# Graph attention in split precision: the turned probabilities of a head pair in 64-row blocks, and the order of a pair's step

## The reference

```python
h = max(layernorm(x), 0)
q, k, v = h @ wq.T + bq, h @ wk.T + bk, h @ wv.T + bv
q2 = (q @ wiq.T + biq).reshape(384, 16, 64).transpose(1, 0, 2)     # k2, v2 alike
scores = einsum('hnd,hmd->hnm', q2, k2) / 8 + mask[None]
attn = softmax(scores, axis=-1)
out = einsum('hnm,hmd->hnd', attn, v2).transpose(1, 0, 2).reshape(384, 1024)
result = x + out @ wo.T + bo
```

## Time and profile before

| | before |
|---|---|
| median of 3 runs | 299.47 us |
| profiled execution, its own time | 299.46 us |
| span in that profile | 297.7 us |
| TensorE busy | 291.4 us, 98% |
| VectorE / ScalarE / GpSimd busy | 177.7 / 153.6 / 148.5 us |
| granted TensorE clock | 1.0 of full speed |
| transposes of probabilities | 144, of 128x128, 272 ns each, overlapping |

### The profile page before, as it was taken

One profiled execution on the slowest core, in us unless ns is written; L12 is line 12 of the kernel. 1 busy time (PEld: TensorE's weight loads), 2 busy tenths in 40 slices (PEclk: granted clock), 3 DMA queues, 4 the chain that ended last, 5 costly groups with the idle time before them and its releaser, 6 DMA issues.

```text
span 297.7 us, 4737 instructions
## 1 busy us (share of the span) xinstructions
PE 291.4 (98%) x1705; PEld 271.6 (91%) x1705; DVE 177.7 (60%) x475; ACT 153.6 (52%) x288; POOL 148.5 (50%) x153
## 2 busy tenths in 40 slices
PE   6999999999999999999999999999999999999996
PEld 3799998888899999999999999999999999888885
DVE  4995988786544443444467665656666666735241
ACT  2874642252532444334434586868686868975100
POOL 5551354643463545544400895657484839884000
PEclk9999999999999999999999999999999999999999
DMA  7948875648743444333554043040404040400032
GB/s 269 329 154 284 280 232 191 219 166 279 285 115 108 132 141 143 109 109 137 186 184 143 0 142 104 40 137 7 141 3 143 1 141 12 167 36 2 0 141 73
DMA packets 15818, 40.84 MB, mean 137 GB/s; under 512 B 3481, under 2 KB 4914, under 8 KB 15794
## 3 DMA queue, kind: packets, MB, share of 16 engines
q1 hardware_dynamic: 13346, 38.53, 38.9%
q0 software_dynamic: 2016, 1.21, 1.4%
q10 hardware_dynamic: 432, 0.79, 0.7%
HBM read 37.71 MB, written 2.81 MB: 136 GB/s over the span
## 4 chain that ended last, share of the span: by engine, by line
PE 89%; DMA 4%; DVE 3%; ACT 2%; issue 0%; POOL 0%; SPq 0%
PE bank L805 25%; PE bank L807 24%; PE bank L806 24%; PE bank L933 5%; PE bank L920 5%; PE bank L949 3%; PE bank L948 3%; DMA raw<-in_slabs 2%; DMA x_sb<-in_x 1%; ACT w_hi L433 1%; DVE stats L640 1%; ACT a_hi L463 1%; DMA key_rows<-key_row 1%; DVE a_lo L686 0%; ACT x_sb L453 0%
## 5 line engine op out<-in xcount | busy, mean ns | idle before, releaser
L386 POOL DMA_INDIRECT cells<-value,cell x51 | 53.1, 1042 | 63.8 <-DMA cells<-value,cell 46.8
L433 ACT ACTIVATE w_hi<-raw 128x1024 fp32r<-128x1024 f32 x51 | 54.1, 1060 | 22.2 <-PE bank L807 17.3
L805 PE MATMUL bank<-a_hi,w_hi 128*128 128x384 f32 x184 | 61.6, 335 | 0.7 <-DVE b_lo L661 0.7
L807 PE MATMUL bank<-a_lo,w_hi 128*128 128x384 f32 x184 | 61.5, 334 | 0.0
L806 PE MATMUL bank<-a_hi,w_lo 128*128 128x384 f32 x184 | 61.5, 334 | 0.0
L673 DVE TENSOR_TENSOR w_lo<-raw,w_hi 128x1024 fp32r<-128x1024 f32 x36 | 44.0, 1223 | 15.6 <-ACT w_hi L433 15.6
L412 POOL TENSOR_SCALAR prob<-prob,row_inv 128x384 f32<-128x384 f32 x36 | 22.7, 642 | 40.1 <-DVE row_inv L740 40.1
L357 POOL TENSOR_TENSOR w_lo<-raw,w_hi 128x1024 fp32r<-128x1024 f32 x15 | 35.9, 2395 | 7.1 <-ACT w_hi L433 7.1
L805 PEld LDWEIGHTS bank<-a_hi,w_hi 128*128 128x128 f32 x184 | 34.5, 188 | 1.1 <-DVE w_lo L673 1.0
L806 PEld LDWEIGHTS bank<-a_hi,w_lo 128*128 128x128 f32 x184 | 34.5, 188 | 0.0
L807 PEld LDWEIGHTS bank<-a_lo,w_hi 128*128 128x128 f32 x184 | 34.5, 188 | 0.0
(11 more groups left out here) (142 smaller groups left out, 609.2 us busy)
## 6 DMA issues: line engine op xcount, KB each, us to landing
raw<-in_slabs SPq DMA_DIRECT2D x56, 512.0 KB, 3.4
work<-key_rows SPq DMA_DIRECT2D x6, 256.0 KB, 6.2
prob<-key_rows SPq DMA_DIRECT2D x6, 256.0 KB, 3.8
x_sb<-in_x SPq DMA_DIRECT2D x3, 512.0 KB, 6.3
out_y<-x_sb SPq DMA_DIRECT2D x5, 256.0 KB, 2.1
cells<-prob SPq DMA_DIRECT2D x2, 576.0 KB, 7.4
cells<-value,cell POOLq DMA_INDIRECT x51, 3.8
x_sb<-in_x ACTq DMA_DIRECT2D x3, 256.0 KB, 4.4
```

What stands on the lines that cost most here:

```text
L386: nc.gpsimd.indirect_dma_start(out=cells[c][:, :], out_offset=bass.IndirectOffsetOnAxis(ap=cell[:, t:t + 1], axis=0), in_=value[:, t:t + 1 ...
L433: nc.scalar.activation(split_place(s)[0], raw[:, s % RAW, :], ACT.Copy).then_inc(slab_hi, 1)
L805: nc.tensor.matmul(psum, w[0], a[0], start=first, stop=False)
L807: return nc.tensor.matmul(psum, w[0], a[1], start=False, stop=last)
```

## The change

- For heads 0 to 11 (`in_halves`), both heads of a pair are turned in one run, `turn_pair`. Each transpose takes 64 rows of a block, so it uses one half of the array: 36 transposes, two by two on the two halves, each with a 64x64 identity moving. Results of the lower and the upper half go to different banks, so a turned block of 384 columns lies in two banks in runs of 64, and the copies read it by `pt_place` and write it in order by `pt_as_placed`.
- On TensorE the key tile stands whole behind the scores; then come the values of the pair before's odd head, the run of transposes, 3/8 of the query tile, the values of the even head, 5/8 of the query tile. The odd head's values wait for the next step.
- On ScalarE all six exponentials stand in a row, then a weight split and the key tile. `half_part` and the copies come after these. VectorE and GpSimd follow the same order.
- The psum banks are one tensor and renumbered; `scores` waits for `pt_lo` of the head two back, the copies for both half banks and for the values that read the buffer before, and the waits of `tile` and of the first `heads_values` are moved by two tiles.
- The last four heads keep the old transposes.

```diff
-            return bank[((0, 1, 7), (2, 5, 6))[h % 2 if h < H - 4 else 0][m]]
+        def in_halves(h):
+            return h < H - 4
+        def pt_place(h, m):
+            if not in_halves(h):
+                return bank[m][:, 0:N]
+            own = slice(h % 2 * NT * D, (h % 2 + 1) * NT * D)
+            return banks[:, 2 * m:2 * m + 2, own].rearrange("p x (n d) -> p x n d", d=D)
...
             def pt_hi_part(h, m):
-                act.wait_ge(pt_done, h * NT + m + 1)
-                nc.scalar.activation(pt_hi[:, m, :], pt_bank(h, m)[:, 0:N], ACT.Copy).then_inc(pt_hi_ok, 1)
+                if in_halves(h):
+                    both = h // 2 * 2 * NT + 2 * (m + 1)
+                    act.wait_ge(pt_done, both)
+                    act.wait_ge(pt_done_high, both)
+                else:
+                    act.wait_ge(pt_done, h * NT + m + 1)
+                if h >= 1:
+                    act.wait_ge(head_done, h)
+                nc.scalar.activation(pt_as_placed(pt_hi, h, m), pt_place(h, m), ACT.Copy).then_inc(pt_hi_ok, 1)
...
             def scores(j, n):
                 turn, m = j % 2, slice(n * P, (n + 1) * P)
+                if j >= 2:
+                    pe.wait_ge(pt_lo_ok, (2 * j - 3) * NT + n + 1)
...
+            def turn_pair(pair):
+                pe.wait_ge(prob_ok, chunk_at(pair, NT - 1, 1) + 1)
+                for m in range(NT):
+                    pe.wait_ge(masked, chunk_at(pair + 1, m, 1) + 1)
+                    for x in range(2):
+                        for n in range(NT):
+                            for high in range(2):
+                                own = slice(high * D, (high + 1) * D)
+                                at = (x * NT + n) * D
+                                mm = nc.tensor.transpose(score_bank(2 * m + high)[:, at:at + D],
+                                                         probs[pair % 2][x][own, n, m * P:(m + 1) * P], ident[own, own])
+                                if n == NT - 1:
+                                    mm.then_inc((pt_done, pt_done_high)[high], 1)
...
             def filler(j, at):
-                if j < PAIRS - 1 and at < 2:
-                    pair_tile(3 * KT + 3 + 2 * j, (range(0, 3), range(3, KT))[at])
+                if j < PAIRS - 1 and at == 0:
+                    pair_tile(3 * KT + 3 + 2 * j)
                 elif j < PAIRS - 2:
-                    pair_tile(3 * KT + 4 + 2 * j)
+                    pair_tile(3 * KT + 4 + 2 * j, (range(0, 3), range(3, KT))[at - 1])
                 elif j == PAIRS - 2:
                     pe.wait_ge(tile_lo, 5 * KT)
-                    out_part(0, range(0, 4))
+                    out_part(0, (range(0, 1), range(1, 4))[at - 1])
...
                 filler(j, 0)
-                if j >= 1:
+                if 2 <= j < PAIRS:
+                    heads_values(h - 1)
+                if j >= 1 and in_halves(h):
+                    turn_pair(j - 1)
+                elif j >= 1:
                     turn_probs(h)
                 filler(j, 1)
                 if j >= 1:
                     heads_values(h)
-                if j >= 1:
-                    turn_probs(h + 1)
+                    if not in_halves(h):
+                        turn_probs(h + 1)
                 filler(j, 2)
-                if j >= 1:
+                if j >= PAIRS - 1:
                     heads_values(h + 1)
```

More of the change, by code:

```diff
@@ L158, in cell_rows @@
             return cells[c][0:N * N, :].rearrange("(t p n) a -> p t (n a)", p=P, n=N)
[L160 to L165, removed]
+        banks = ctx.enter_context(nc.psum_tensor("banks", [P, 8, HALF], F32))
+        bank = [banks[:, i, :] for i in range(8)]
+        h_bank = [bank[4], bank[7], bank[3], bank[5], bank[0], bank[1], bank[2], bank[4]]
+        tile_bank = bank[6:8]
+        v2_bank = [bank[3:6], bank[0:3]]
+        pair_bank = bank[6]
+        head_bank = bank[7]
         cut = HALF + HALF // 2
[L169 to L171 removed]
+        out_pieces = [(0, n, slice(0, HALF), bank[b][:, :]) for n, b in enumerate((6, 3, 4))]
+        out_pieces += [(1, n, slice(HALF, F), bank[b][:, :]) for n, b in enumerate((5, 0))]
+        out_pieces += [(1, 2, slice(HALF, cut), bank[1][:, 0:cut - HALF]), (1, 2, slice(cut, F), bank[2][:, 0:F - cut])]
         edges_in, rows_in, small_in, y_in = sem("edges_in"), sem("rows_in"), sem("small_in"), sem("y_in")
@@ L418, in _ @@
                 norm_part(j, 1)
-                if j >= 2:
+                if in_halves(2 * j - 2):
+                    norm_part(j, 2)
+                    for s in first:
+                        split_lo(s)
+                    if j >= 2:
+                        pair_lo_part(j - 2)
+                else:
                     pair_lo_part(j - 2)
-                for s in first:
-                    split_lo(s)
-                norm_part(j, 2)
+                    for s in first:
+                        split_lo(s)
+                    norm_part(j, 2)
                 for s in second:
@@ L535, in _ @@
                     exp_part(j, 1)
+                if in_halves(h):
+                    exp_part(j, 2)
+                    for s in first:
+                        split_hi(s)
+                    tile_hi_part(3 * KT + 3 + 2 * j)
+                if j >= 2:
+                    half_part(h - 1)
                 if j >= 1:
@@ L540, in _ @@
                     pair_hi_part(j - 2)
[L541 to L544, removed]
-                if j >= 1:
+                if in_halves(h):
+                    for s in second:
+                        split_hi(s)
+                    if j >= 1:
+                        for m in range(NT):
+                            pt_hi_part(h + 1, m)
+                        half_part(h)
+                    if j < PAIRS - 2:
+                        tile_hi_part(3 * KT + 4 + 2 * j)
+                else:
+                    for s in first:
+                        split_hi(s)
                     half_part(h)
-                if j < PAIRS:
-                    exp_part(j, 2)
-                if j >= 1:
+                    if j < PAIRS:
+                        exp_part(j, 2)
                     for m in range(NT):
                         pt_hi_part(h + 1, m)
-                for s in second:
-                    split_hi(s)
-                if j < PAIRS - 2:
-                    tile_hi_part(3 * KT + 4 + 2 * j)
+                    for s in second:
+                        split_hi(s)
             half_part(H - 1)
@@ L777, in _ @@
                     y_part(2)
+                if in_halves(h):
+                    inv_part(j, 2)
+                    tile_lo_part(3 * KT + 3 + 2 * j)
+                if j >= 2:
+                    head_part(h - 1)
                 if j >= 1:
@@ L782, in _ @@
                     pair_lo_part(PAIRS - 2)
-                if j < PAIRS - 1:
-                    tile_lo_part(3 * KT + 3 + 2 * j)
-                if j >= 1:
+                if in_halves(h):
+                    if j >= 1:
+                        for m in range(NT):
+                            pt_lo_part(h + 1, m)
+                        head_part(h)
+                    if j < PAIRS - 2:
+                        tile_lo_part(3 * KT + 4 + 2 * j)
+                else:
                     head_part(h)
-                if j < PAIRS:
-                    inv_part(j, 2)
-                if j >= 1:
+                    if j < PAIRS:
+                        inv_part(j, 2)
                     for m in range(NT):
                         pt_lo_part(h + 1, m)
-                if j < PAIRS - 2:
-                    tile_lo_part(3 * KT + 4 + 2 * j)
             head_part(H - 1)
```

34 lines of the change are left out of this document (16 added, 18 removed).

## The result

The changed kernel takes 296.60 us (median of 9 runs, 296.19 to 298.51) against 299.54 for the kernel before (median of 9 runs beside it). The ratio is 0.9914, 95% interval 0.9895 to 0.9933: faster by 0.9%. The prediction said 296.0 us; its direction holds, and the measured 2.9 us stand against 3.5 predicted. The profiled execution took 296.3 us (span 294.6), 3.16 us less than that of before.

A forecast was written before the change was run, and what follows sets the result against it. The prediction took TensorE's instruction stream to bound the kernel. From 299.46 us it took 3.5 for shorter transpose runs and added 0.1 for a step 6 wait, giving 296.1, written as 296.0 us; range 295.0 to 299.9.

The forecast's parts named there:

- TensorE's stream is the time: Whole kernel: TensorE busy 291.4 of 297.7 us, so a microsecond off its stream before the last matmul shortens the kernel equally.
- A whole transpose is bound by its moving side, a half one by its load: Transposes: 128 moving columns take 0.109 us; a double half transpose takes 0.06 us, set by its 128-column load.
- the lower bound: Double half transpose: at least 0.055 us, the halved moving stream, for a run of 1.37 us and a gain of 4.0 us.
- Side by side: Run of transposes: two 64-row blocks on the array's two halves go together, making 36 transposes 18 double ones.
- The run at 1.45 us: Transposes of each pair: 1.45 us against 2.03 now, gaining 0.58 us a pair, 3.5 us over six pairs.
- direct reading: Old transposes on TensorE's timeline: nine cost 0.98 us, said to agree with 2.03 us a pair.
- The order hides and gives nothing: New order on TensorE: the count of matmuls is the same, so only new waits can cost; steps 1 to 5 nothing.
- Step 6: 0.1 us, at most 0.5: Step 6: odd head's pt_lo comes just in time for the scores of pair 7; a loss of 0.1 us, at most 0.5.
- Cover before the even values, 1.0 and 0.5 us: Steps 1 to 5: turned blocks ready before the even head's values want them, first by 1.0 us, last by 0.5.
- Before the scores: Steps 1 to 5: odd head's last pt_lo ends at 13.3, wanted by the next scores at 14.9, covered by 1.6 us.
- Copies from two banks: nothing: Copies on ScalarE and VectorE: reading two banks in runs of 64 costs zero extra, staying at 490 and 550 ns.
- Rival D's supply, 43 ns an instruction: Run of transposes: 72 instructions at 43 ns each take 3.1 us, a run of 3.5, time 308; rival's chance 0.11.

The follow-up runs named there:

- e11: The changed kernel with all 18 half transposes of the lower rows first, then all 18 of the upper rows: 303.64 us, ratio 1.0109.
- e10: The changed kernel with half transposes that load only 64 of 128 columns and take only 32 of 64 rows: 293.43 us, ratio 0.978.
- e4: The changed kernel with two runs of 18 half transposes, one per head, three query tile matmuls between them: 300.4 us, ratio 1.0015.
- e8: The changed kernel with two more 384-column copies on ScalarE ahead of the even head's pt_hi copies, in steps 1 to 6: 298.91 us, ratio 0.9959.
- e12: e1 with only 64 of the 128 columns of each block loaded, all 128 identity columns still moving: 300.18 us, ratio to the kernel before 1.0005.
- e5: The changed kernel with each half transpose taking 32 of its 64 rows, so 32 columns move and 128 are loaded: 296.35 us, ratio 0.9887.
- e6: The changed kernel with each half transpose loading 64 of 128 columns and still moving 64: 295.65 us, ratio 0.9847.
- e1: The changed kernel's order, but each pair turned by 18 whole 128x128 transposes in one run: 300.11 us, ratio to the kernel before 0.9995.
- e2: The changed kernel's half blocks and single run per pair, with every engine in the order of the kernel before: 301.0 us, ratio 1.0042.

## Why the prediction was right, point by point

**TensorE's stream is the time.** Right: steps with TensorE busy throughout before and after, and where nothing new waits a change of the run appears whole in the step (0.55 less in the changed kernel than before; against the changed kernel +0.93 in e11, -0.56 in e10). In e4 and e8 the waits for the copies come on top.

**A whole transpose is bound by its moving side, a half one by its load.** Right, both: e12 leaves 0.109 with half the load, e5 leaves 0.062 with half the moving columns, e6 brings 0.055 for 64 moving columns, the figure of the lower bound. The 0.06 us read from two loads after an idle stretch carried the forecast, and 0.062 came. The Trainium skill, "TensorE: Matmul & The Clock Gate", section "LDWEIGHTS (loading the stationary operand)", has a load as columns / 1.2, 107 ns here. The pairs at 0.062 us speak against it for these f32 blocks.

**Side by side.** Right, and looser than thought: the two transposes of a pair need not be issued one right behind the other. Even 18 after 18 (e11) cost 0.93 us a step, less than the 1.1 of no overlap at all.

**The run at 1.45 us.** It is 1.47, so the steps fall by 0.55 where 0.58 was said. The prediction called its direct reading of the old transposes, 0.98 us for nine, in agreement with 2.03 a pair; twice 0.98 is 1.96, and most of the rest is the slower slots behind each run of nine. The 2.03 was the right number to subtract from. Net of the 0.1 us for step 6 the prediction had 3.4 us; the profile has 3.16. The run is 6 x 0.03 = 0.2 of the difference, step 6 another 0.1, and the two ends of the kernel give 0.07 back. That the medians are only 2.9 apart is within their scatter.

**The order hides and gives nothing.** Right (e1). Why it is needed the prediction did not say. It looked at what the new order could cost; e2 shows what the old one would: 0.6 us a step on the tiles' one psum bank.

**Step 6: 0.1 us, at most 0.5.** The size is near, 0.2 (0.55 - 0.34), but the place was wrong. The prediction put the loss before the scores of pair 7, where pt_lo was in time by 0.1 us and nothing was lost. The 0.19 us went before the even head's values: the prediction named the cause, only three matmuls of output work ahead of them, and gave it no price. That 0.2 lies so near 0.1 is luck.

**Cover before the even values, 1.0 and 0.5 us.** The first is right (pt_lo done at 204.32 + 0.55 = 204.87, wanted at 205.95). The second was a miscount: the last block is wanted four slots after the first, not two, so the cover is 0.8 us by the timeline and 0.75 by e8. Before the scores: the last pt_lo ends at 207.79 + 1.49 = 209.28, and the scores that want it come six slots and the way in after 209.68, at 210.8: 1.5 us, where 1.6 was said.

**Copies from two banks: nothing.** Right, 490 and 550 ns, as before (490 and 551).

**Rival D's supply, 43 ns an instruction.** Far off: e10 passes 36 loads and 36 matmuls in 0.77 us, 11 ns each. How many of them had been queued before, the trace does not show, so this is the pace at which they pass, not a measured supply. The densest stretch that a trace happens to show is no bound. The Trainium skill ("TensorE: Matmul & The Clock Gate", section "Wait — 56ns, not 53.3ns?") gives the sequencer about 62 ns per matmul, with hardware decode off. That did not bind either: the 36 of the changed kernel pass in 1.34 us, where 36 x 62 ns are 2.2.

## What to carry to other kernels

Short matmuls have two prices, the load of the stationary side and the passing of the moving side; find which one is later before halving the other. One pair of loads after an idle stretch told it here. In this kernel half-array work pays 0.4 us for going in and out, so it is worth collecting: one run per pair gained 0.55 us a step, two runs 0.06, partly because the copies came later. A wait that a view puts down to an engine is not yet lost time: compare the distance between the instructions with the same distance where nothing waits (step 6). And when a run gets shorter, ask which bank or copy it was hiding: without the new order the same half blocks made the kernel slower.

## What the runs showed of the hardware

- The two halves of the array take up their instructions apart. With groups of six or eighteen for one half, the other starts three before the end of the group (0.18 and 0.92 us late at 0.062 us each).
- A 64-row f32 transpose takes 0.062 us with 128 columns loaded and 64 or 32 moved, 0.055 with 64 and 64, 0.032 with 64 and 32. A 128-row one takes 0.109 us with 128 or 64 columns loaded.
- A second run of 64-row transposes in a step, and so a second way in and out, cost 0.35 us (e4).
- On ScalarE two more copies of 384 f16 columns (e8) pushed what stood behind them by 1.07 us, where 0.38 us each was reckoned from copies out of psum. Why they do not overlap as those do stays open.
